# First layer of a graph network on one core: GpSimd's source product behind VectorE's destination product, ScalarE's probability copies at the head of its list

## What is computed

```python
# layer 0, per graph; 12 heads of 64
h        = einsum('bnd,ade->bane', x, W)
th       = tanh(h)
attn     = einsum(th, w_src) + swapaxes(einsum(th, w_dst), 2, 3)   # source + destination term
attn     = softmax(where(adj, leaky(attn), -999))
feat     = elu(attn @ h + b)
gate     = sigmoid(x @ H_w.T + H_b)
x        = layernorm(x + gate * feat + (1 - gate) * x)
# layer 1: six-head masked attention with q, k, v, f projections, residual, layernorm
```

## Time and profile before

| | |
|---|---|
| median of 3 runs | 3150.84 us (3149.88 to 3152.88) |
| the profiled execution: time | 3151.22 us |
| its span | 3149.3 us |
| first layer, stretch 30 to 1183 us | PE busy 1021.54, DVE 1043.05, ACT 543.30, POOL 569.28 |
| second layer, 1183 us to the end | PE busy 1876.10, DVE 792.56 |
| granted TensorE clock over the span | 0.984 |

### The profile page before, as it was taken

How to read it: one execution, slowest core, us unless ns; L and a number is a source line. 1 busy time by engine, 2 the same in 40 slices (tenths; PEclk the granted TensorE clock), 3 DMA queues, 4 the chain that set the end, 5 groups by cost and what they waited for, 6 DMA issues and landing times.

```text
span 3149.3 us, 55422 instructions
## 1 busy us (share of the span) xinstructions
PE 2913.6 (93%) x21696; PEld 2654.5 (84%) x21696; DVE 1848.3 (59%) x3271; ACT 1105.8 (35%) x2661; POOL 687.3 (22%) x329
## 2 busy tenths in 40 slices
PE   7989899898998963999999999999999999999998
PEld 6777677777776752999999999999999999999998
DVE  6999999999999974344344344344334434334333
ACT  4444544445444443222222232232232222232232
POOL 2454554545545450000000000000000000000000
PEclk9999999999999986999999999999999999999999
DMA  4222232222222224001001001001001001000000
GB/s 137 87 88 89 86 96 86 90 86 86 96 86 92 85 76 151 21 21 42 21 21 42 21 21 42 21 21 42 21 21 42 22 21 34 29 22 32 31 21 21
DMA packets 88931, 170.80 MB, mean 54 GB/s; under 512 B 34496, under 2 KB 34496, under 8 KB 88768
## 3 DMA queue, kind: packets, MB, share of 16 engines
q1 hardware_dynamic: 88768, 168.24, 16.6%
HBM read 117.48 MB, written 50.72 MB: 53 GB/s over the span
## 4 chain that ended last, share of the span: by engine, by line
PE 56%; DVE 3%; ACT 2%; DMA 1%; issue 0%; SPq 0%; DVEq 0%; ACTq 0%
PE L_ps_k L105 13%; PE L_ps_q L105 13%; PE L_ps_a L105 13%; PE L_ps_a L912 11%; PE L_ps_c L895 2%; PE L_ps_s L875 2%; ACT L_probs L658 1%; DVE L_cT_lo L744 1%; ACT L_cT_hi L644 1%; PE L_ps_q L827 0%; PE L_ps_s L827 0%; PE L_ps_k L827 0%; PE L_ps_pt L882 0%; DVE L_logits L720 0%; DVE L_neg_max L726 0%
## 5 line engine op out<-in xcount | busy, mean ns | idle before, releaser
L616 POOL TENSOR_TENSOR L_x_tok<-L_x_tok,L_bf_all 128x768 f32<-128x768 f32 x64 | 116.5, 1842 | 1775.5 <-PE L_ps_s L827 1775.5
L442 PE MATMUL L_ps_hg<-L_w_hi,L_xT_hi 128*128 128x512 f32 x1152 | 473.4, 411 | 25.2 <-DVE L_h_one L407 13.2
L442 PE MATMUL L_ps_hg<-L_w_hi,L_xT_lo 128*128 128x512 f32 x1152 | 456.5, 396 | 0.0
L442 PE MATMUL L_ps_hg<-L_w_lo,L_xT_hi 128*128 128x512 f32 x1152 | 456.0, 396 | 0.0
L105 PE MATMUL L_ps_k<-L_xT_hi,L_w_hi 128*128 128x256 f32 x1152 | 331.9, 288 | 0.0
L105 PE MATMUL L_ps_q<-L_xT_hi,L_w_hi 128*128 128x256 f32 x1152 | 328.1, 285 | 0.0
L105 PE MATMUL L_ps_k<-L_xT_hi,L_w_lo 128*128 128x256 f32 x1152 | 326.2, 283 | 0.0
L105 PE MATMUL L_ps_k<-L_xT_lo,L_w_hi 128*128 128x256 f32 x1152 | 325.7, 283 | 0.0
L105 PE MATMUL L_ps_q<-L_xT_lo,L_w_hi 128*128 128x256 f32 x1152 | 325.6, 283 | 0.0
L105 PE MATMUL L_ps_q<-L_xT_hi,L_w_lo 128*128 128x256 f32 x1152 | 325.4, 282 | 0.0
L442 PEld LDWEIGHTS L_ps_hg<-L_w_hi,L_xT_hi 128*128 128x128 f32 x1152 | 217.7, 189 | 87.1 <-issue 33.3
(11 more groups left out here) (106 smaller groups left out, 6447.0 us busy)
## 6 DMA issues: line engine op xcount, KB each, us to landing
L_x_tok<-x SPq DMA_DIRECT2D x64, 384.0 KB, 3.1
L_dst_all<-dst_scratch SPq DMA_DIRECT2D x128, 192.0 KB, 3.3
L_x_res<-x SPq DMA_DIRECT2D x64, 384.0 KB, 3.8
x_scratch<-L_y_out SPq DMA_DIRECT2D x64, 384.0 KB, 2.6
L_x_tok<-x_scratch SPq DMA_DIRECT2D x32, 768.0 KB, 4.2
out<-L_x_tok SPq DMA_DIRECT2D x32, 768.0 KB, 3.4
L_stage<-W SPq DMA_DIRECT2D x6, 384.0 KB, 5.7
L_stage<-H_t SPq DMA_DIRECT2D x6, 384.0 KB, 7.1
```

What stands on the lines that cost most here:

```text
L442: ins = pe.matmul(ps_hg[:, cols], xT[a][c], w[bb][c], start=(c == 0 and n == 0), stop=(c == KC - 1 and n == 2))
L616: pool.tensor_tensor(x_tok[:, s, t], x_tok[:, s, t], bf_all[:, :], ALU.add).then_inc(biased, 1)
```

## The change

Two lists of the first layer are written in another order, and one wait is another. In POOL's list the source product of tile T stands ahead of the three operations of tile T-3, and it waits for `thdst_done` (DVE's destination product of the same tile) where it waited for `tanh_done`. In ACT's list the four probability copies of tile T-2 stand first, ahead of the gate and the doubled residual. PE's, DVE's and SP's lists are the same as before.

```diff
 POOL
             def step(T, u, has):
+                if has(0):
+                    pool.wait_ge(thdst_done, T + 1)
+                    if has(-1):
+                        pool.wait_ge(src_done, T)
+                    pool.tensor_tensor(th_src[:, :], th[:, :], wsrc_all[:, :], ALU.mult).then_inc(thsrc_done, 1)
                 if has(-3):
...
                     pool.tensor_tensor(y_out[:, slot, :], y_out[:, slot, :], delta[:, :], ALU.add).then_inc(y_done, 1)
-                if has(0):
-                    pool.wait_ge(tanh_done, T + 1)
...
 ACT
             def step(T, u, has):
+                if has(-2):
+                    act.wait_ge(pt_done, T - 1)
...
+                            ins = act.copy(out[:, :, :, parity, :], pair[:, :, :, graph(g)])
+                    ins.then_inc(ptc_done, 1)
                 if has(-1):
                     g = gate[:, (u - 1) % 4, :]
                     act.wait_ge(z_done, T)
...
                     act.mul(y_out[:, slot, :], x_res[:, slot, :], 2.0).then_inc(x2_done, 1)
-                if has(-2):
-                    act.wait_ge(pt_done, T - 1)
...
```

More of the change, by code:

```diff
@@ L270, in step @@
                     pool.tensor_tensor(y_out[:, slot, :], y_out[:, slot, :], delta[:, :], ALU.add).then_inc(y_done, 1)
-                if has(0):
-                    pool.wait_ge(tanh_done, T + 1)
-                    if has(-1):
-                        pool.wait_ge(src_done, T)
-                    pool.tensor_tensor(th_src[:, :], th[:, :], wsrc_all[:, :], ALU.mult).then_inc(thsrc_done, 1)
             steps(pool, step, NT + 3)
@@ L289, in step @@
             def step(T, u, has):
+                if has(-2):
+                    act.wait_ge(pt_done, T - 1)
+                    if has(-3):
+                        act.wait_ge(pv_done, T - 2)
+                    for parity in range(2):
+                        for g in range(2):
+                            out = probsT[graph(g), :, :].rearrange("p (b c two) n -> p b c two n", b=2, two=2)
+                            pair = banks(ps_t)[graph(parity), :, :].rearrange("p b (c n) -> p b c n", c=KC // 2)
+                            ins = act.copy(out[:, :, :, parity, :], pair[:, :, :, graph(g)])
+                    ins.then_inc(ptc_done, 1)
                 if has(-1):
```

## The result

The changed kernel takes 3446.47 us (median of 4, 3440.13 to 3448.71) against 3150.36 for the kernel before, a recorded ratio of 1.0935, 95% interval 1.0916 to 1.0954. The forecast was 3465 with a range of 3395 to 3525. The profiled execution has a span of 3438.2 us (time 3440.13), 288.9 more than before; the first layer ends near 1476 us instead of 1183 (+293), the second takes 1962 us where it took 1966. One execution of a later run (the source product's old wait) was in a slow state, 3647.57 us at a granted clock of 0.744 over its span, and is left out of that run's median.

What follows compares the result with a forecast made beforehand. PE and DVE were nearly full in a 17.86 us step; the new circle through POOL, SP and dst's DMAs takes 23.0. Sixty steps above 17.82 give +311, with the ends +314 on 3151.2: 3465 us, range 3395 to 3525.

Steps and rivals of the forecast that it cites:

- The turn behind step 63: After the last looped step, L366 comes 15.5 us after L390 instead of 6.84: +8.7, less 2.3 without POOL's contention.
- ELU waits for the subtraction, L419 wants the port at 5.7: ACT's ELU starts at 3.9 us after L390's end; DVE's L419 then waits until 5.9 for POOL's gate product.
- The rival in which POOL wins the port: POOL's addition starts before DVE's L419 and ends 0.6 us earlier a step: 3429 us, chance 10%.
- The store of `dst` is held up by that of `y_out`: On SP's queue, dst lands 2.8 us after y_out's issue, and cannot report before y_out has landed (2.6).
- The rival without queueing: dst's store is not held up by y_out's: 1.0 us less in 60 steps, 3405 us, chance 7%.
- The term of 2.8: Time from y_out's issue to dst's landing, 2.8 us, taken from adj's load landing behind x's.
- PE has about 7 us of slack: PE has work for 16 of the 23.0 us step, so brief clock drops in its gaps cost nothing.
- part (a): ACT's copies move ahead of three operations, aimed at PE's 1.58 us wait; works, but worth nothing as PE isn't the bound.
- PE waits 3 to 4 us each for exp and for L407: Expected sign: PE idles twice a step, before the probability transposes (18.4 to 22) and before block 0 (22.9 to 26.1).
- SP's wait at the store of `y_out` grows to some 7 us: Expected sign: SP's wait for y_done grows from small to some 7 us a step; its dst_done wait vanishes.
- If the gain came through, 3055: Rival: the DMA chain stays hidden, PE bounds the step at 16.2 us, 3055 us; chance 3%.
- Its point of decision: L366 must start by 10.3 us after L390 for no loss, 8.7 for the whole gain; the forecast chain has 15.5.

Runs made afterwards that it cites:

- the source product's old wait: Changed kernel with POOL's source product waiting for tanh_done again, both lists still turned: 3360.34 us, 1.0661.
- the copies' part alone: Kernel before with only the probability copies moved first in ACT's list: 3143.07 us, 0.9983.
- POOL's part alone: Kernel before with only POOL's new list order and wait, ACT's list as before: 3440.05 us, 1.0925.
- the extra matmuls: Changed kernel with 25 matmuls a step, whose result nothing reads, added in PE's two idle times: 3454.39 us, 1.0978.
- the two stores exchanged: Changed kernel in which SP still waits for y_done first, but then issues the store of dst before that of y_out: 3367.67 us, 1.0702.
- SP's edit: Kernel before with dst's store, its wait and the dst_all loads put ahead of y_out's store in SP's list: 3148.97 us, 1.0002.
- the fast kernel: Changed kernel with dst's store, its wait and the dst_all loads put ahead of y_out's store in SP's list: 3013.13 us, 0.9565.

## Why the prediction was right

The kernel is slower by the mechanism that was named, and the size came out within 6% of the difference (+314 forecast, +296 between the medians; +289 on the profiled executions). Term by term, as means over steps 4 to 63 of the changed kernel's timeline:

| term | forecast | measured |
|---|---|---|
| L390's end to SP's store of `y_out` (POOL's four operations) | 8.4 | 8.22 (8.17 to 8.35) |
| from there to the loads of `dst_all` | 2.8 + 0.1 | 2.81 (2.51 to 3.68) |
| loads' issue to L366 | 4.2 | 4.26 (3.79 to 5.06) |
| L366 to L390's end | 7.5 | 7.40 |
| step | 23.0 | 22.70 |

L390's end in step 3 moved from 80.15 to 75.93 (-4.2, forecast -3.8), and from there to step 63 (1437.78) the loop takes 1361.85 us instead of 1069.15: +293, forecast +311. The turn behind step 63 adds 5.2 (forecast 6.4), and the rest of the program, which the change doesn't touch, came out 4.8 shorter (forecast nothing). So the forecast's excess of 25 us on the profiled execution is 18 from the loop, 2 from its two ends and 5 from the rest. No run says why the untouched rest is shorter.

- *ELU waits for the subtraction, L419 wants the port at 5.7.* It started at 5.5 (624.13), behind a wait of 0.70. The rival in which POOL wins the port didn't come: POOL's gate product ended at 624.29, L419 at 625.10, the addition 1.72 later, which is the turn-taking read from the earlier trace rows.
- *The store of `dst` is held up by that of `y_out`*: yes, by 0.8 us a step (2.36 against 1.57). The rival without queueing was priced at 1.0 us a step. The term of 2.8 was taken from loads of another size and direction, so that it came out at 2.81 owes something to luck.
- *PE has about 7 us of slack and part (a) is worth nothing*: the copies' part alone and POOL's part alone show it, and the extra matmuls show that the time of the fallen clock lay in the slack.
- *PE waits 3 to 4 us each for exp and for L407*: for L407 it is 3.08, for exp only 1.50 (79.4 in 53 steps). The forecast had PE idle from 18.4 on; block 0 at the low clock takes 1.4 us longer, so PE is through at 19.8 (638.44), and exp is done at 21.4 and not 22. Neither has an effect on the sum.
- *SP's wait at the store of `y_out` grows to some 7 us*: a misreading, though with no effect on the sum. It was clocked from `dst_done`; the wait began when SP had issued the last load of the step before, so it is 16.8 us a step.
- *If the gain came through, 3055*: this was 42 us too high, for PE's work of a step is 15.6 us and not 16.2. Its point of decision (L366 by 10.3 us after L390 for no loss) fits the runs, though none comes near it: L366 starts 6.7 us after L390's end with `dst` first, and the kernel is fast; it starts at 14.1 with the two stores exchanged and at 15.3 in the changed kernel, and both are slow.

## What to carry to other kernels

When an operation is moved later in its engine's list, follow its semaphore to every queue that waits on it and list what stands behind that wait, above all in a queue of DMAs that serves two chains: here the store of `y_out`, which nothing waits for soon, held up the store of `dst`, behind which DVE waits in every step. Put the transfer on the recurring path ahead of the one that only drains. And try the parts of a change together as well as apart: POOL's turned list, the early copies and SP's edit are worth +9%, -0.2% and 0 alone, and -4.3% together.

## What the runs showed of the hardware

The granted clock falls to 0.50 in each step of the changed kernel behind two idle times of 1.19 and 3.08 us with 0.87 us of transposes between them, where the loop before, with gaps of 1.6 us, stays at 1.00 (2.4 GHz). The prediction had left open whether it would. With ACT's part alone PE has one gap of 1.95 us in most steps, and the clock does not do the same each time: behind the gap that ends at 617.46 it is 0.50 from 619 to 621 us, when block 0 was already running; behind the next such gap, which is 1.94 us and ends at 652.89, it stays at 1.00. So the length of a gap by itself did not decide it.

PE's busy time of a step, read from the loop before, is 16.06 us, and PE needs 15.6 when nothing makes it wait. The ends of matmuls are modelled in the profile. Ahead of block 0 it shows an idle time of 0.20 us, while the stretch from the transposes to block 0 is 0.45 longer than in the fast kernel (1.02 against 0.57); ahead of the transposes of x it shows 1.60, while the stretch is 1.75 longer. The 0.4 us between are counted as busy. A busy sum is not the time that the engine needs when nothing makes it wait.
